# Transposing the second normalised activation by a DMA on the sync queue instead of on TensorE

## What is computed

```python
x = x + layernorm(attn(layernorm(x), Wq, Wk, Wv, Wo))
x = x + layernorm(ffn(layernorm(x), weight, aux1, aux2, bias))

def attn(x):                      # per head, 16 heads of 64
    qf, kf, v = phi(x @ Wq), phi(x @ Wk), x @ Wv      # phi = elu + 1
    kv, z = kf.T @ v, kf.sum(tokens)
    return ((qf @ kv) / (qf @ z + 1e-6)) @ Wo
def ffn(x):
    return tanh(x @ weight @ aux1 @ aux2 + bias)
```

## Time and profile before

| | us |
|---|---|
| median of two runs | 1035.0 |
| the two runs | 1031.31 and 1038.69 |
| the profiled execution | 1031.6 |
| its span on the slowest core (core 5), from first to last instruction | 1030.0 |
| spans of the eight cores | 1021.9 to 1030.0 |

### The profile page before, as it was taken

The page is one execution under the profiler, slowest core; times in us unless marked ns, Lnnn a source line. Parts: engine busy times, 40 slices in busy tenths (PEclk is TensorE's granted clock), DMA queues, the critical chain, the costliest instruction groups (busy, mean ns, idle before and its releaser), DMA issues.

```text
span 1030.0 us, 10964 instructions; the slowest of 8 cores (1021.9 to 1030.0 us)
## 1 busy us (share of the span) xinstructions
PE 607.2 (59%) x3392; PEld 310.7 (30%) x3392; DVE 540.1 (52%) x914; ACT 452.5 (44%) x769; POOL 213.7 (21%) x130
## 2 busy tenths in 40 slices
PE   0520557774575765775686555555657658755753
PEld 0310443232232332332332344332323323322321
DVE  1430533224665675566666545346655756676653
ACT  1922991002343353342533799832533533435333
POOL 3255000001132313222312200001222231233132
PEclk9965679997766876777778666758768767877677
DMA  6868410000111111011103232001111111111001
GB/s 192 277 230 260 128 42 1 0 1 1 42 48 55 42 61 62 21 62 62 61 21 123 99 118 82 30 1 40 42 62 41 62 50 33 62 42 58 4 41 41
DMA packets 20507, 69.52 MB, mean 67 GB/s; under 512 B 1873, under 2 KB 4049, under 8 KB 20450
## 3 DMA queue, kind: packets, MB, share of 16 engines
q1 hardware_dynamic: 11490, 35.27, 10.5%
q0 software_dynamic: 6784, 25.17, 6.7%
q10 hardware_dynamic: 2176, 8.39, 2.6%
HBM read 52.04 MB, written 16.78 MB: 67 GB/s over the span
## 4 chain that ended last, share of the span: by engine, by line
PE 32%; ACT 23%; DVE 22%; issue 11%; DMA 5%; POOL 5%; DVEq 1%; ACTq 0%; SPq 0%; POOLq 0%
PE PS_C L720 11%; PE PS_B L760 6%; DVE big_b L736 4%; DVE ln_bn L472 4%; POOL big_b L696 3%; DVE ln_bn L470 3%; PE PS_C L613 3%; PE PS_C L627 3%; ACT big_b L498 2%; DVE big_b L692 2%; ACT xn_tm L498 2%; ACT big_b L772 2%; DMA stage<-wo 2%; PE PS_A L671 2%; DVE big_b L493 2%
## 5 line engine op out<-in xcount | busy, mean ns | idle before, releaser
L481 ACT ACTIVATE ln_l<-ln_ag,eps_s 128x1 f32<-128x1 f32 x128 | 38.1, 298 | 320.3 <-DVE ln_ag L474 287.7
L760 PE MATMUL PS_B<-p_b,big_b 128*128 128x512 bf16 x512 | 151.1, 462 | 27.9 <-DVE big_b L749 27.9
L696 POOL TENSOR_TENSOR big_b<-big_b 128x1024 bf16<-128x1024 bf16 x32 | 74.4, 2325 | 441.5 <-DVE big_b L692 405.2
L720 PE MATMUL PS_C<-wo_b,big_b 128*128 128x512 bf16 x512 | 160.4, 483 | 3.4 <-ACT big_b L710 3.4
L781 POOL TENSOR_TENSOR out_b<-big_b 128x1024 f32<-128x1024 f32 x32 | 78.8, 2463 | 294.2 <-DVE big_b L493 282.9
L704 PE MATMUL PS_A<-big_b,kvblk_b 128*128 128x128 bf16 x256 | 33.3, 273 | 105.8 <-POOL big_b L696 82.5
L760 PEld LDWEIGHTS PS_B<-p_b,big_b 128*128 128x128 bf16 x512 | 56.3, 115 | 125.7 <-issue 93.0
L520 PE MATMUL PS_T<-eye_b,xn_tm 128*128 128x128 bf16 x256 | 30.4, 292 | 104.0 <-ACT xn_tm L498 65.2
L720 PEld LDWEIGHTS PS_C<-wo_b,big_b 128*128 128x128 bf16 x512 | 58.2, 119 | 95.3 <-issue 66.6
L560 DVE SCALAR_TENSOR_TENSOR kf_b<-relu_b,exp_b 128x1024 bf16<-128x1024 bf16 x32 | 40.9, 1278 | 72.6 <-ACT exp_b L553 60.4
L736 DVE TENSOR_TENSOR big_b<-x_tm,big_b 128x1024 f32<-128x1024 f32 x32 | 59.7, 1866 | 35.3 <-ACT big_b L498 30.0
(11 more groups left out here) (70 smaller groups left out, 1075.9 us busy)
## 6 DMA issues: line engine op xcount, KB each, us to landing
x_tm<-x SPq DMA_DIRECT2D x64, 512.0 KB, 3.3
y<-out_b POOLq DMA_DIRECT2D x32, 512.0 KB, 3.0
stage<-a POOLq DMA_DIRECT2D x8, 1024.0 KB, 6.8
stage<-wt ACTq DMA_DIRECT2D x4, 1024.0 KB, 6.6
stage<-wo ACTq DMA_DIRECT2D x4, 1024.0 KB, 6.4
stage<-wkvblk SPq DMA_DIRECT2D x2, 512.0 KB, 7.2
stage<-wqblk SPq DMA_DIRECT2D x1, 512.0 KB, 8.3
stage<-eye SPq DMA_DIRECT2D x1, 64.0 KB, 1.7
```

The lines of the kernel that those rows point to most:

```text
L696: p.op("gpsimd", lambda e: e.tensor_tensor(qf2_b[j], qf_b[j], rdenbc_b[j], ALU.mult), reads=[("qf", j), ("rdenbc", j, 0), ("rdenbc", j, 1) ...
L720: p.op("tensor", lambda e, cc=c, h2=hh: e.matmul(PS_C[:, h2 * 512:(h2 + 1) * 512], ctx_b[j][:, cc * 128:(cc + 1) * 128], wo_b[:, cc * 1024 ...
L760: p.op("tensor", lambda e, cc=c, h2=hh: e.matmul(PS_B[:, h2 * 512:(h2 + 1) * 512], xn2f_b[j][:, cc * 128:(cc + 1) * 128], p_b[:, cc * 1024 ...
```

## The change

In stage B the eight transposes on TensorE and the VectorE copy go, and one DMA with `transpose=True`, issued by the sync engine from SBUF to SBUF, writes `xn2f` from `xn2tm`. It moves 128 partitions of 1024 bf16 elements (256 KB), in eight blocks of 128 columns: out[n, c, p] = in[p, c, n]. The reads and writes declared for the planner are those of the old pair; the helper `dma` gets the new argument. Pass 1 keeps its transposes on TensorE.

```diff
-    def dma(engine, out_ap, in_ap, reads=(), writes=()):
-        return p.op(engine, lambda e, o=out_ap, i=in_ap: e.dma_start(out=o, in_=i),
+    def dma(engine, out_ap, in_ap, reads=(), writes=(), transpose=False):
+        return p.op(engine,
+                    lambda e, o=out_ap, i=in_ap, tr=transpose: e.dma_start(
+                        out=o, in_=i, transpose=tr),
                     reads=reads, writes=writes, dma=True)
...
-        cl = new_cluster()
-        for c in range(NCH):
-            p.op("tensor", lambda e, cc=c: e.transpose(
-                PS_T[:, cc * 128:(cc + 1) * 128],
-                xn2tm_b[j][:, cc * 128:(cc + 1) * 128], eye_b[:]),
-                 reads=[("xn2tm", j), ("eye",)], writes=[("PT",)], cluster=cl)
-        p.op("vector", lambda e: e.tensor_copy(xn2f_b[j], PS_T[:]),
-             reads=[("PT",)] + g0, writes=[("xn2f", j)])
+        dma("sync", xn2f_b[j].rearrange("p (c n) -> p c n", n=128),
+            xn2tm_b[j].rearrange("p (c n) -> p c n", n=128),
+            reads=[("xn2tm", j)] + g0, writes=[("xn2f", j)], transpose=True)
```

## The result

The changed kernel takes 1085.3 us (median; runs from 1083.2 to 1090.8), the kernel before, run beside it, 1033.3 us. The ratio is 1.050, with a 95% interval from 1.048 to 1.052. Forecast was 1009. The time lies inside the range given, but on the other side of "no change", near the 1087 of rival 2.

The account below looks back on a forecast made before the run. No engine was saturated; a chain over two tiles in pass 2 set the pace. Profiled 1031.6 - 13.0 (removed pieces) - 17.5 (`out` reordered) + 4.3 (end) = 1005.4; runs' median lies 3.4 higher: 1009 us, range 975 to 1115.

Parts of the forecast that it names:

- rival 2: Planner's order still carries the DMA latency, on GpSimd or by a VectorE tie: 52 us slower, 1087 us; chance 0.22.
- What bounds the kernel: No engine above 59% of the span; the time lies in chains, a pass 2 loop taking 40.6 us for two tiles.
- The landing, D = 6 us: Each tile's transposing DMA in pass 2 was taken to land in 6 us, with bounds of 1.7 and 12.3.
- The queue: Sync engine's queue is free; x loads and transposes don't block each other in steady state; costed at nothing.
- If D is below 11.2, TensorE does not wait for it: Planner prices the DMA at 11.2 us and places `p_b`'s matmuls 8.3 us later, so other tiles' work covers shorter landings.
- `out` moves behind the product, 17.5 us gained: On GpSimd, `out` of tile t falls behind tile t+2's product: 2.9 us a turn, six turns; lower bound nothing.
- The removed pieces, 13.0 us: Pass 2's transposes (8.1 us) and VectorE copies (4.9 us) on the chain go, 13.0 us gained if the DMA is hidden.
- The end, +4.3 us: After the last tile nothing covers the DMA: 4.3 us more with a 6 us landing, 10.6 with 12.3.
- The first sequence's end is covered by pass 1 of the second: At the turn between sequences, the second sequence's pass 1 covers the first one's DMA at its end; no cost in the sum.
- The prediction's last sentence: Forecast falls if the landing far exceeds all bounds, or the new order, not derived step by step, is otherwise worse; unsized.
- The clock: TensorE's granted clock, 0.74 and 0.76 in pass 2's windows, was left as it is, with no term in the sum.

Follow-up runs that it names:

- E11: Changed kernel in its own order, every transposing DMA issued twice, one behind the other: 1137.8 us, some 52 more than the changed kernel.
- E2: Order planned for the changed kernel, each DMA then replaced by the TensorE transposes and copy, copy's place chosen by hand: 1096.8 us, ratio 1.060 to the kernel before.
- E1: Order planned for the kernel before, the transposing DMA then put in place of transposes and copy: 1048.1 us, ratio 1.013 to the kernel before.
- E3: Changed kernel with the planner's price of the transposing DMA set to 3.4 us instead of 11.2: 1111.9 us, ratio 1.074 to the kernel before.
- E9: Kernel before, same instructions, another set of planner prices (transpose 80 ns, cheaper matmul overhead, activations and handoff, window 300): ratio 0.921 to the kernel before.
- E10: Order of E9, the DMA then put in place of transposes and copy: 945.6 us, ratio 0.917 to the kernel before.
- E6: Kernel before, same instructions; only the planner is told the copy's result comes 8.3 us later: 1103.9 us, ratio 1.068.
- E7: Kernel before, same instructions; only the planner is told stage B's eight transposes and the copy take no time: 1066.1 us, ratio 1.033.

## Why the prediction was wrong, step by step

- **What bounds the kernel: right.** No engine was saturated, and a loop over two tiles set the pace. With 26 and 34 us less work on two engines the span grew all the same.
- **The landing, D = 6 us: too long.** It is 3.1 us. The bounds 1.7 and 12.3 held. The nearest row by number of runs (8.3 us for wqblk) misled. The Trainium skill ("DMA: Bandwidth & Descriptors", Latency and other measured facts) has 261 GB/s for transposes with a non-contiguous middle dimension, from which I estimate 1.0 us for 256 KB; by that estimate 2.1 of the 3.1 us would be fixed, and no run here separates the two parts. The other figure that I weighed, the 1309 ns that the Trainium skill ("VectorE: DVE Perf Modes", The three transpose paths) has for one 128x128 block, does not scale to eight: that would be an estimate of 10.5 us, and the measurement decides for 3.1.
- **The queue: right.** In the turn shown the DMA started 0.14 us after its input was ready (408.14 + 0.81 = 408.95, issued at 409.09). The loads of x did not hold it up there, and VectorE waited 22.9 us in all for loads of x, against 23.7 before.
- **"If D is below 11.2, TensorE does not wait for it": this step failed.** The planner's allowance is in modelled time, and it does not move the matmuls by an amount; it sorts everything anew. In the changed kernel a landing ended TensorE's wait in 17 turns, 44.9 us in all (16.6 of them in the first drain), with D at 3.1. E11 shows that there was no slack: each added microsecond came back in 17 turns.
- **"`out` moves behind the product, 17.5 us gained": this step failed too.** GpSimd did leave the chain (1%, from 5%), and the product is back at 2123 ns from 2325. But the gain was taken by the tie on VectorE, which I had named in rival 2, and had given as lower bound "nothing" where the bound should have been a loss. The loop grew from 42.1 to 44.3 us in the turns shown. The sum had no term for a new order that is worse without any latency; E2, which has the new order and no transposing DMA, measures it: 62 us, of which the copy's place may be a part. The prediction's last sentence had named this as what would make it fall, and gave it no price.
- **The removed pieces, 13.0 us: gone, but outweighed.** They left the chain, and 57.7 us of DMA pieces came in, 44.7 more; the span grew by 51.3. The two numbers lie near each other, but the one is not the cause of the other: with the old pair in the same order (E2) the kernel is 11 us slower still.
- **The end, +4.3 us: the term was mis-sized with D.** From the last tile's L495 (1057.74) to its matmuls (1061.01) passed 3.3 us instead of 1.7, so 1.6 more.
- **"The first sequence's end is covered by pass 1 of the second": this step failed.** It was put at nothing; the stretch around it grew by 11.4 us, over a fifth of the loss, by the drain shown with the result.
- **Rival 2 had the nearest number, by luck, and half of the mechanism.** Its signs were mostly there: a tie on VectorE, DMA pieces in the chain, a landing under 11 us, and a spacing of 21.6, just short of its 22. But it put the whole loss on the latency, twelve turns at D = 6, and reached 1087 that way; the chain has seventeen turns at 3.1. With the measured D its own sum, 12 x (3.1 + 0.1 - 1.8), is 17 us, or 1052: that fits E1 (1048), where the order was held, and misses the change, and E2 is no faster with no transposing DMA in it. So the order carries the loss, and not what the DMA takes longer than the old pair. I argued against the rival with "the planner knows the latency", and E3 shows that a price nearer the truth made the order worse.
- **The clock: right.** Its mean on the slowest core was 0.763 before and is 0.755, and a matmul with `p_b` takes 467 ns on average instead of 462, one with Wo 465 instead of 483; so it is no main cause here. In the good orders it rises (0.81 to 0.85 on the cores of E9 and E10), and how much of their gain is the clock's is not separated.

What stays open: why the greedy planner writes bad orders once the pair is out of its input. E6 and E7 separate two causes in its input, but no single tie was taken away in an experiment, so the tie on VectorE is read from the chains of the changed kernel and of E2, and not shown to be the one that counts.

## What to carry to other kernels

When a planner writes the order, an edit to one operation is an edit to every queue: hold the order fixed and change the work, then hold the work fixed and change the order, before a number is put down to the operation itself. Count the turns in which the operation stands in the chain: that count times the latency added came near what more latency cost in a fixed order (17 and 11 turns), though it did not tell whether the operation beats the one it replaces (E10 against E9). An allowance in a cost model bought nothing. And try other prices in the planner before tuning an operation: the order was worth 8% here, the transposes about 1% either way.

## What the hardware showed that I had not expected

- A transposing DMA of 256 KB from SBUF to SBUF lands 3.1 us after its issue starts (3.0 to 5.2 over 32), and issuing it takes the sync engine 1237 ns, where a plain 512 KB load takes it 328 ns:

```profile
L402 SPq DMA_DIRECT2D x_tm<-x x64: 327/328/624, 12.0 to 969.2; - x64
L402 SPq DMA_TRANSPOSE big_b<-big_b x32: 1232/1237/1756, 264.1 to 1057.8; - x32
```

- It makes about 1056 packets: the packets went from 20507 to 54297 for 32 of them. The loads of x, on the same queue, land in 4.0 us instead of 3.3.
- VectorE's residual add takes 1.22 us when GpSimd does nothing beside it, and 3.1 us where GpSimd's bf16 product of another tile runs beside it for 2.0 us, as in the turn of the earlier trace rows; in the one case before where only GpSimd's `out` (f32) ran beside it, for 0.92 us, it took 1.21. On average it is 1866 ns before, 1706 in the changed kernel, 1290 in E9 and 1654 in E10, with the same instruction.
